# Half of FFN 2's down product from GELU values in two fp32r parts, and new orders of all engines

## The chip, the core and the metric

The kernel runs on one core of a Trainium2 chip. The core's engines are TensorE (PE in the profile; its weight loads are PEld), VectorE (DVE), ScalarE (ACT), GpSimd (POOL) and SyncE (SP), which issues the DMAs. Each engine runs its own instructions in the order in which the program gives them and waits for the others through semaphores. The metric is the device time of one execution in microseconds (us), lower being better.

## The reference, cut to what matters

Four layers, each adding to x (128 sequences, 32 steps, 128 channels). Layer 0, a mixture of experts, comes first; layers 1 to 3 each have a recurrent part over the 32 steps and a feed-forward part (FFN). The change is in FFN 2, and in the order of everything in layers 1 to 3.

```python
x = x + L0_ffn(L0_cond(x))          # experts
x = x + L1_ffn(L1_cond(x))          # LSTM; quantised linear, 3-tap convolution, silu, quantised linear
x = x + L2_ffn(L2_cond(x))          # h = tanh(h @ Wh + x @ Wx + b); the FFN below
x = x + L3_ffn(L3_cond(x))          # gate = sigmoid(h @ Wh.T + z @ Wz.T + b); h = tanh(h * leak + gate * z)

def L2_ffn(x, W1, b1, W2, b2):      # 128 -> 512 -> 128, W1 and W2 ternary (-1, 0, 1)
    h = einsum('bsd,fd->bsf', x, ternary(W1)) + b1
    h = gelu(h, approximate=False)
    return einsum('bsf,df->bsd', h, ternary(W2)) + b2
```

## The kernel before

Everything up to about 318 us of the span is layer 0 with its preparations. The rest, some 235 us, is one fused stage in which the layers 1, 2 and 3 run as a pipeline over the 32 steps t: step t of the LSTM stands beside earlier steps of the later layers. Values are held with channels on the 128 partitions and the 128 sequences along the row.

Steps go in pairs (p, or blocks v of two steps; the last two steps are blocks 15 and 16 of one step each). One loop of the program (`for q in range(FILL, TURNS)`) is called a turn below: two LSTM steps and two steps, or one block, of everything else. What each engine does per turn:

- **TensorE**: `gate_x` and `gate_h` (LSTM gates, lines 1663 and 1673), `turn_h` and `turn_q1` (transposes, 1685 and 1690), `up_tap` (three products per step for the convolution, 1700 and 1701, fp32r), `down1` (bf16, 1709), `turn_y` (1715), `rnn` (layer 2's recurrence, 1722 and 1723), `up2` (FFN 2 up, in two fp32r parts of h2, 1748 and 1749), `down2` (FFN 2 down, 1759, f32), `leaky` (layer 3's recurrence, 1772 and 1773), `mix_products` (1786 and 1787) and `value` (1793).
- **VectorE**: LSTM cell (`gate_products` 1914, `new_cell` 1920, `new_h` 1927), maxima and scales of both quantisations (1933 to 1945, 1980 to 1993), the convolution's three sums per step `conv_next`, `conv_here`, `conv_last` (1951, 1959, 1966), `silu` (1974), the residual sums `new_x2` (1998) and `new_x3` (2003), layer 3's `gated3` (2009) and `leaked3` (2014), and `shift_diff`, `mix`, `gated_value`, `result` (2023 to 2044).
- **ScalarE**: the tanh of every gate and state, both roundings, `scale_y` (1858), `gelu` (1874), `tanh_gate3` (1883) and `tanh_state3` (1888).
- **GpSimd**: `split_h2` alone, once per pair: a cast of h2 to fp32r (2054) and the difference to it (2056).

No scheduler works here. `pe_program`, `act_program` and `dve_program` write the order of each engine out by hand: a prologue, the loop of turns, and an epilogue. An engine that waits at one step holds up all behind it. FFN 2's GELU values lie in one buffer `g2` of 4 x 2 x 128 columns. `down2(v)` writes to bank 3, which `up2` uses too, so `up2(v, 0)` waits for `new_x3(v - 1)` and `gelu(v, ...)` for `down2(v - 1)`. The program has a fixed distance between the LSTM and the later layers: turn q has `gate_h` of steps 2q-3 and 2q-2, `down2(q-7)`, `leaky` of 2q-16 and 2q-15, `mix_products(q-10)` and `value(q-11)`.

## Time and profile before

| | us |
|---|---|
| median of 3 runs | 554.79 (554.44 to 554.80) |
| profiled execution | 554.63 |
| its span (first to last instruction) | 553.3 |
| TensorE busy in the span | 540.1 (98%) |
| VectorE busy | 425.7 (77%) |
| ScalarE busy | 380.6 (69%) |
| GpSimd busy | 197.8 (36%) |

The profiled execution lies 0.16 us under the median. Its span is 1.3 us shorter than its time; this part lies outside the first and last instruction. The TensorE clock was granted in full (1.00 in every stretch shown below). A busy TensorE means that a matmul is in flight; the distance from one matmul's start to the next says what it costs while the engine is saturated. On VectorE and ScalarE, too, the busy times of neighbours overlap by under 0.1 us, so a sum of starts is a little under a sum of busy times.

### The profile page before, as it was taken

Reading aid. Unit: us, or ns where it says so; the run is one execution under the profiler, and the core shown is the slowest. Engines: PE = TensorE matmul, PEld = TensorE weight load, DVE = VectorE, ACT = ScalarE, POOL = GpSimd, SP = SyncE. Lnnn points to the kernel's source line nnn. Section 1 sums busy time; section 2 is a strip of 40 time slices with the busy share of each in tenths; the row PEclk is TensorE's granted clock in tenths of the full one; section 3 lists DMA queues with packets and bytes.
Section 4 is the critical chain, followed back from the end, with each engine's and each line's share of the span. In section 5 each row is a group of like instructions: output and inputs, shape, how many; then the busy total and the mean of one; then the engine's idle time right before and its main releaser. Section 6 shows DMA issues by size and latency. Waiting matters only on the chain.

```text
span 553.3 us, 10078 instructions
## 1 busy us (share of the span) xinstructions
PE 540.1 (98%) x3341; PEld 468.0 (85%) x3341; DVE 425.7 (77%) x1026; ACT 380.6 (69%) x857; POOL 197.8 (36%) x186
## 2 busy tenths in 40 slices
PE   8999999999999999999999989999999999999997
PEld 7877888887887899999999877788989999987785
DVE  4987656567659779676856359998999999999866
ACT  4567767758767664454552246888988888888965
POOL 4688788788788402947100000010000000000100
PEclk9999999999999999999999999999999999999999
DMA  8634306512081302021000000122111111112211
GB/s 285 194 152 159 152 1 230 191 56 97 2 305 43 124 10 82 1 73 62 2 1 1 0 1 2 20 39 21 21 20 20 21 31 30 34 38 47 45 52 39
DMA packets 30227, 37.36 MB, mean 68 GB/s; under 512 B 20096, under 2 KB 23648, under 8 KB 29280
## 3 DMA queue, kind: packets, MB, share of 16 engines
q1 hardware_dynamic: 30176, 36.72, 21.2%
q8 instruction: 28, 0.46, 0.4%
q14 instruction: 23, 0.19, 0.1%
HBM read 30.24 MB, written 2.28 MB: 59 GB/s over the span
## 4 chain that ended last, share of the span: by engine, by line
PE 81%; DVE 12%; ACT 4%; issue 2%; POOL 1%; DVEq 0%; ACTq 0%
PE bank L325 11%; PE bank L1248 10%; PE bank L327 10%; PE bank L326 10%; PE bank L1673 4%; PE bank L1759 4%; PE bank L1663 4%; PE bank L1700 3%; PE bank L1701 3%; PE bank L1316 2%; PE bank L1198 1%; PE bank L1748 1%; PE bank L1786 1%; PE bank L409 1%; PE bank L1772 1%
## 5 line engine op out<-in xcount | busy, mean ns | idle before, releaser
L387 POOL TENSOR_TENSOR hidden_low<-hidden,hidden_high 128x512 fp32r<-128x512 f32 x72 | 94.4, 1318 | 24.6 <-ACT hidden_high L372 22.4
L2054 POOL CAST h_high<-h 128x256 fp32r<-128x256 f32 x15 | 6.4, 426 | 197.6 <-ACT h L1865 191.2
L452 ACT ACTIVATE bank<-bank 128x512 f32<-128x512 f32 x56 | 32.6, 583 | 34.5 <-PE bank L327 34.3
L456 DVE TENSOR_TENSOR hidden<-bank,big 128x512 f32<-128x512 f32 x56 | 38.5, 688 | 15.8 <-ACT bank L452 14.6
L372 ACT CAST hidden_high<-hidden 128x512 fp32r<-128x512 f32 x70 | 43.0, 615 | 3.3 <-DVE hidden L456 1.9
L1700 PE MATMUL bank<-taps_high,q1T 128*128 128x512 f32 x94 | 42.9, 457 | 1.0 <-ACT q1T L1828 0.6
L325 PE MATMUL bank<-xin_high,sw_high 128*128 128x256 f32 x128 | 43.9, 343 | 0.0
L1701 PE MATMUL bank<-taps_low,q1T 128*128 128x512 f32 x94 | 37.1, 395 | 0.0
L1382 DVE COPY yT<-bank 128x256 f32<-128x256 f32 x32 | 13.6, 424 | 30.4 <-PE bank L1248 30.4
L1801 ACT ACTIVATE gates_t<-bank,lstm_b_half 128x128 f32<-128x128 f32 x96 | 28.2, 364 | 12.2 <-PE bank L1673 8.8
L1663 PE MATMUL bank<-x,lstm_wx 128*128 128x128 f32 x256 | 34.4, 277 | 1.7 <-ACT gates_t L1801 0.9
L326 PE MATMUL bank<-xin_low,sw_high 128*128 128x256 f32 x128 | 36.1, 282 | 0.0
L327 PE MATMUL bank<-xin_high,sw_low 128*128 128x256 f32 x128 | 35.9, 280 | 0.0
L1663 PEld LDWEIGHTS bank<-x,lstm_wx 128*128 128x128 f32 x256 | 32.0, 191 | 4.4 <-ACT gates_t L1801 3.3
L1442 ACT ACTIVATE pb<-bank 128x512 f32<-128x512 f32 x32 | 19.5, 608 | 22.7 <-PE bank L327 22.7
L1673 PE MATMUL bank<-hL,lstm_wh 128*128 128x128 f32 x256 | 34.1, 276 | 0.5 <-DVE hL L1927 0.4
L1673 PEld LDWEIGHTS bank<-hL,lstm_wh 128*128 128x128 f32 x256 | 32.3, 192 | 2.4 <-DVE hL L1927 1.4
L998 POOL TENSOR_TENSOR hidden_low<-hidden,hidden_high 128x512 fp32r<-128x512 f32 x24 | 30.8, 1287 | 9.4 <-ACT hidden_high L778 9.0
L1248 PE MATMUL bank<-pb,w 128*128 128x256 f32 x128 | 32.8, 378 | 0.0
L1248 PE MATMUL bank<-th,w 128*128 128x256 f32 x128 | 32.7, 378 | 0.0
L1759 PE MATMUL bank<-g,ffn_w 128*128 128x256 f32 (+1 forms) x136 | 30.7, 368 | 0.0
L1874 ACT ACTIVATE g<-bank,ffn_b 128x256 f32<-128x256 f32 (+1 forms) x68 | 27.6, 467 | 1.0 <-PE bank L1749 0.6
(270 smaller groups left out, 1736.6 us busy)
## 6 DMA issues: line engine op xcount, KB each, us to landing
big<-gates_scratch SPq DMA_DIRECT2D x7, 2048.0 KB, 8.1
w<-in_f_w SPq DMA_DIRECT2D x16, 256.0 KB, 6.2
onehot<-topi_scratch SPq DMA_DIRECT2D x8, 512.0 KB, 4.2
outT<-x SPq DMA_DIRECT2D x15, 128.0 KB, 2.1
xT<-in_xT SPq DMA_DIRECT2D x3, 512.0 KB, 7.4
hidden<-in_ffn_w SPq DMA_DIRECT2D x3, 256.0 KB, 5.2
hidden<-in_conv_w SPq DMA_DIRECT2D x3, 256.0 KB, 4.8
xT<-in_xT SPq DMA_DIRECT2D x2, 256.0 KB, 4.2
```

The costliest lines, as they stand in the source:

```text
L325: pe.matmul(dst, wh[:, cols], vh[:, :], start=start, stop=False)
L326: pe.matmul(dst, wh[:, cols], vl[:, :], start=False, stop=False)
L327: return pe.matmul(dst, wl[:, cols], vh[:, :], start=False, stop=stop)
L372: act.copy(hidden_hl[u % 3][0][:, :], hidden[u % 3][:, :]).then_inc(s_hi, 1)
L387: pool.tensor_tensor(hidden_hl[u % 3][1][:, :], hidden[u % 3][:, :], hidden_hl[u % 3][0][:, :].bitcast(F32), ALU.subtract).then_inc(s_lo, 1)
L456: dve.tensor_tensor(hidden[u % 3][:, :].rearrange("p (i k) -> p i k", k=P), r_bank[j % 2][:, :].rearrange("p (i k) -> p i k", k=P), gate_r ...
L1248: mm = pe.matmul(y_bank[e % 2][:, 0:SLOT_GE], w2[:, e, ht, :], hb[w % 4][:, i * SLOT_GE:(i + 1) * SLOT_GE], start=(ht == 0), stop=(ht == H ...
L1663: mm = pe.matmul(gate_ps(t, q), lstm_wx[:, q * P:(q + 1) * P], x1[:, t, :], start=(0 < t < EARLY or (t > 0 and q == 0)), stop=(t == 0), sk ...
L1673: mm = pe.matmul(gate_ps(t, q), lstm_wh[:, q * P:(q + 1) * P], hL[:, (t - 1) % 2, :], start=(t == 0), stop=(t > 0), skip_group_check=True)
L1700: pe.matmul(dst, q, taps_high[:, 2 - j, :], start=True, stop=False)
L1701: pe.matmul(dst, q, taps_low[:, 2 - j, :], start=False, stop=True).then_inc(c_taps, 1)
L1759: mm = pe.matmul(bank_down(v), ffn2_w2[:, f, :], part(g2[:, f, :, :], v), start=(f == 0), stop=(f == HT - 1))
```

## The change

1. `down2(v)` for blocks 0 to 12 (`SPLIT = 13`): of the four row blocks f of the hidden layer, f = 0 and 1 are multiplied in f32 as before; f = 2 and 3 are multiplied in fp32r twice, once with the rounded GELU values `g2_high` and once with the rest `g2_low`. Blocks 13 to 16 stay in f32.
2. ScalarE makes `g2_high` by one copy of 128x512 per block (`split_g_high`), GpSimd makes `g2_low` by one subtraction of 128x512 (`split_g_low`). The subtraction waits for `g2_high`, for `down2(v - 2)` and for VectorE's `conv_next(2v + 10)`.
3. `g2` becomes a ring of three buffers, so `gelu(v, ...)` waits for `down2(v - 3)` only. `down2(v)` moves from bank 3 to the free half of bank 6, which holds `leaky`'s result: `up2(v, 0)` now waits for `gelu(v - 1, 1)`, not for `new_x3(v - 1)`, and `down2(v)` waits for `new_x3(v - 1)` and for `tanh_gate3` of step 2v - 1.
4. The factor of FFN 1's second weight moves from `m2w` (a VectorE instruction per pair, line 1992, gone) into `new_x2`, which becomes a scalar_tensor_tensor of the same shape.
5. `ffn2_w2` is written as fp32r from a raw copy of its own; f32 products read it through a bitcast.
6. GpSimd no longer splits the one-step pair 15, whose result no product read (`split_h2` for p = 0 to 14).
7. The orders of TensorE, ScalarE and VectorE are written anew. FFN 2's down product and all of layer 3 stand one block later against the LSTM: the loop has `gate_h` of 2q-2 and 2q-1, `down2(q-8)`, `leaky` of 2q-17 and 2q-16, `mix_products(q-11)`, `value(q-11)`.

```diff
@@ up2
                         elif v:
-                            pe.wait_ge(c_x3, v)
+                            pe.wait_ge(c_g2[1], v)
@@ down2
                     pe.wait_ge(c_g2[0], v + 1)
-                    pe.wait_ge(c_g2[1], v + 1)
+                    if v < SPLIT:
+                        pe.wait_ge(c_glow, v + 1)
+                    else:
+                        pe.wait_ge(c_g2[1], v + 1)
+                    if v == 0:
+                        pe.wait_ge(c_to, EARLY)
+                    elif v < PAIRS:
+                        pe.wait_ge(c_x3, v)
+                        pe.wait_ge(c_g3, 2 * v)
                     for f in range(HT):
-                        mm = pe.matmul(bank_down(v), ffn2_w2[:, f, :], part(g2[:, f, :, :], v),
-                                       start=(f == 0), stop=(f == HT - 1))
+                        if v < SPLIT and f >= 2:
+                            pe.matmul(bank_down(v), ffn2_w2[:, f, :], g2_high[:, v % 2, f - 2, :, :], start=False, stop=False)
+                            mm = pe.matmul(bank_down(v), ffn2_w2[:, f, :], g2_low[:, v % 2, f - 2, :, :],
+                                           start=False, stop=(f == HT - 1))
+                        else:
+                            mm = pe.matmul(bank_down(v), ffn2_w2[:, f, :].bitcast(F32), part(g2[:, ring(v), f, :, :], v),
+                                           start=(f == 0), stop=(f == HT - 1))
@@ gelu
-                    if v:
-                        act.wait_ge(c_down, min(v, PAIRS))
+                    if v >= RING:
+                        act.wait_ge(c_down, min(v, PAIRS) - RING + 1)
@@ new steps
+            def split_g_high(v):
+                if 0 <= v < SPLIT:
+                    act.wait_ge(c_g2[1], v + 1)
+                    if v >= 2:
+                        act.wait_ge(c_down, v - 1)
+                    act.copy(g2_high[:, v % 2, :, :, :], g2[:, ring(v), 2:HT, :, :]).then_inc(c_ghigh, 1)
+            def split_g_low(v):
+                if 0 <= v < SPLIT:
+                    pool.wait_ge(c_ghigh, v + 1)
+                    if v >= 2:
+                        pool.wait_ge(c_down, v - 1)
+                    if 2 * v + SPLIT_STEP < T:
+                        pool.wait_ge(c_conv, 3 * (2 * v + SPLIT_STEP))
+                    pool.tensor_tensor(g2_low[:, v % 2, :, :, :], g2[:, ring(v), 2:HT, :, :], g2_high[:, v % 2, :, :, :].bitcast(F32),
+                                       ALU.subtract).then_inc(c_glow, 1)
@@ inverse_hs, new_x2
-                    dve.tensor_scalar(m2w[:, 2 * p:2 * p + 2], m2[:, 2 * p:2 * p + 2], half_ws2[:, 0:1], None, ALU.mult)
-                    dve.tensor_tensor(x1[:, t, :], x1[:, t, :], ps_yT, ALU.add).then_inc(c_x2, 1)
+                    dve.scalar_tensor_tensor(x1[:, t, :], ps_yT, half_ws2[:, 0:1], x1[:, t, :], ALU.mult, ALU.add).then_inc(c_x2, 1)
@@ pe_program, in the loop
-                    down2(q - 7)
+                    down2(q - 8)
@@ pool_program
-                for p in range(PAIRS):
+                for p in range(PAIRS + 1):
                     split_h2(p)
+                    split_g_low(p - 1)
```

TensorE in the middle of a turn, around `down2`, before:

```order
L1663 MATMUL bank0<-x1,lstm_wx 128x128 x4
L1722 MATMUL bank7<-x1,rnn_wx 128x128
L1723 MATMUL bank7<-h2,rnn_wh 128x128
L1759 MATMUL bank3<-g2,ffn2_w2 128x256 x4
L1690 MATMUL bank4<-ident,v1 128x128 x2
L1709 MATMUL bank7<-ffn1_w2,q2T 128x128 x4
```

And the same place of the changed kernel:

```order
L1736 MATMUL bank7<-x1,rnn_wx 128x128
L1737 MATMUL bank7<-h2,rnn_wh 128x128
L1786 MATMUL bank6<-g2,ffn2_w2 128x256 x2
L1782 MATMUL bank6<-g2_high,ffn2_w2 128x256
L1783 MATMUL bank6<-g2_low,ffn2_w2 128x256
L1782 MATMUL bank6<-g2_high,ffn2_w2 128x256
L1783 MATMUL bank6<-g2_low,ffn2_w2 128x256
L1677 MATMUL bank0<-x1,lstm_wx 128x128 x4
L1704 MATMUL bank4<-ident,v1 128x128 x2
L1723 MATMUL bank7<-ffn1_w2,q2T 128x128 x4
```

Two of the four f32 products have become four fp32r ones, `gate_x` (lstm_wx) stands behind `down2` and not ahead of it, and the block that is multiplied here is one earlier.

VectorE in the second half of a turn, around the convolution of an even step, before (`products` and `gates_t` are the LSTM's `gate_products` and `new_cell`, `hL` its `new_h`; `z`, `tap1` and `tap0` are the convolution's sums):

```order
L1951 SCALAR_TENSOR_TENSOR z<-bank1,m1,tap1 128x512
L1914 SCALAR_TENSOR_TENSOR products<-gates_t 128x256
L1998 TENSOR_TENSOR x1<-x1,bank7 128x128
L1920 SCALAR_TENSOR_TENSOR gates_t<-products 128x128
L1959 SCALAR_TENSOR_TENSOR tap1<-bank2,m1,tap0 128x512
L2009 SCALAR_TENSOR_TENSOR p3<-g3,x1 128x128
L1927 SCALAR_TENSOR_TENSOR hL<-gates_t,tc 128x128
```

And in the changed kernel, where GpSimd's new subtraction is let go by the end of the first row:

```order
L1985 SCALAR_TENSOR_TENSOR z<-bank1,m1,tap1 128x512
L1948 SCALAR_TENSOR_TENSOR products<-gates_t 128x256
L1993 SCALAR_TENSOR_TENSOR tap1<-bank2,m1,tap0 128x512
L1954 SCALAR_TENSOR_TENSOR gates_t<-products 128x128
L2000 SCALAR_TENSOR_TENSOR tap0<-bank1,m1,tap_bias 128x512
L2042 SCALAR_TENSOR_TENSOR p3<-g3,x1 128x128
L1961 SCALAR_TENSOR_TENSOR hL<-gates_t,tc 128x128
```

`gates_t` now stands behind a convolution sum, and a second one stands between it and `hL`.

TensorE behind `rnn(31)`, the last step of layer 2's recurrence, before (each pair of `leak_wz` and `leak_wh` is one `leaky`):

```order
L1722 MATMUL bank7<-x1,rnn_wx 128x128
L1723 MATMUL bank7<-h2,rnn_wh 128x128
L1793 MATMUL bank5<-kk,ffn3_wv 128x256
L1772 MATMUL bank6<-x1,leak_wz 128x128
L1773 MATMUL bank6<-h3,leak_wh 128x128
L1751 MATMUL bank3<-h2,ffn2_w1 128x128 x2
L1751 MATMUL bank1<-h2,ffn2_w1 128x128 x2
L1751 MATMUL bank0<-h2,ffn2_w1 128x128 x2
L1786 MATMUL bank5<-xr,ffn3_wr 128x256
L1787 MATMUL bank5<-xk,ffn3_wk 128x256
L1772 MATMUL bank6<-x1,leak_wz 128x128
L1773 MATMUL bank6<-h3,leak_wh 128x128
```

And in the changed kernel:

```order
L1736 MATMUL bank7<-x1,rnn_wx 128x128
L1737 MATMUL bank7<-h2,rnn_wh 128x128
L1799 MATMUL bank6<-x1,leak_wz 128x128
L1800 MATMUL bank6<-h3,leak_wh 128x128
L1765 MATMUL bank0<-h2,ffn2_w1 128x128 x2
L1786 MATMUL bank6<-g2,ffn2_w2 128x256 x4
L1820 MATMUL bank5<-kk,ffn3_wv 128x256
L1799 MATMUL bank6<-x1,leak_wz 128x128
L1800 MATMUL bank6<-h3,leak_wh 128x128
L1813 MATMUL bank5<-xr,ffn3_wr 128x256
L1814 MATMUL bank5<-xk,ffn3_wk 128x256
```

The first `leaky` behind `rnn(31)` was that of step 28 and is that of step 27 now; `down2(14)` has come behind `rnn(31)`.

## Rows read from the trace of the kernel before

**Rows 1.** Windows: busy us and (x instructions) of each engine, clock, DMA.
```profile
core 0: us, PE busy (x) PEld busy (x) DVE busy (x) ACT busy (x) POOL busy (x), PEclk, DMA share, GB/s
317.00:372.20 55.20, 50.92 (x362) 42.95 (x362) 45.88 (x111) 39.78 (x106) 1.33 (x3) 1.00 0.08 15
372.20:492.80 120.60, 120.60 (x871) 108.80 (x870) 112.84 (x287) 106.42 (x287) 12.49 (x20) 1.00 0.15 26
492.80:520.50 27.70, 26.20 (x172) 21.72 (x171) 27.54 (x67) 24.99 (x65) 3.06 (x6) 1.00 0.19 43
520.50:553.40 32.90, 28.29 (x180) 23.68 (x178) 21.11 (x62) 21.57 (x66) 1.58 (x3) 1.00 0.16 45
```
**Rows 2.** Chain that ended last, 384 to 450 us: start, us, what.
```profile
384.65 1.73 PE bank L1759 x8
...
396.72 1.73 PE bank L1759 x8
...
436.38 1.73 PE bank L1759 x8
...
439.07 0.43 PE bank L1793 x2
...
445.16 0.43 PE bank L1786 x2
445.60 0.43 PE bank L1787 x2
...
449.73 1.73 PE bank L1759 x8
```
**Rows 3.** Windows of one early and one full turn; columns as in rows 1.
```profile
384.65:396.72 12.07, 12.07 (x91) 10.98 (x91) 11.47 (x29) 11.00 (x29) 1.12 (x2) 1.00 0.12 24
```
```profile
436.38:449.73 13.35, 13.35 (x97) 12.07 (x97) 12.51 (x33) 11.69 (x33) 1.27 (x2) 1.00 0.18 32
```
**Rows 4.** Timeline of TensorE, 504 us: start, us, instruction (up2's four products).
```profile
504.59 0.28 PE L1748 MATMUL bank<-h_high,ffn_w 128*128 128x256 f32 x1
...
505.06 0.40 PE L1700 MATMUL bank<-taps_high,q1T 128*128 128x512 f32 x1
```
**Rows 5.** Groups by line: out<-in, shapes, xcount, busy us, mean ns.
```profile
L387 POOL TENSOR_TENSOR hidden_low<-hidden,hidden_high 128x512 fp32r<-128x512 f32 x72 | 94.4, 1318 | 24.6 <-ACT hidden_high L372 22.4 <-DVE hidden_high L382 1.1
...
L372 ACT CAST hidden_high<-hidden 128x512 fp32r<-128x512 f32 x70 | 43.0, 615 | 3.3 <-DVE hidden L456 1.9 <-DVE hidden L448 1.0
```
**Rows 6.** Timeline, VectorE and GpSimd, 436 to 438 us.
```profile
436.09 0.22 DVE L1992 TENSOR_SCALAR m2w<-m,half_ws 128x2 f32<-128x2 f32 x1
...
436.22 0.16 DVE L1993 RECIPROCAL sc<-m 128x2 f32<-128x2 f32 x1
...
437.68 0.88 POOL L2056 TENSOR_TENSOR h_low<-h,h_high 128x256 fp32r<-128x256 f32 x1
...
437.88 0.82 DVE L2014 SCALAR_TENSOR_TENSOR pre<-h,leak,p 128x128 f32<-128x128 f32 x1
```
**Rows 7.** Timeline, 502 to 504 us: VectorE beside GpSimd's difference.
```profile
503.06 0.73 POOL L2056 TENSOR_TENSOR h_low<-h,h_high 128x256 fp32r<-128x256 f32 x1
503.30 0.47 DVE L2003 SCALAR_TENSOR_TENSOR x<-bank,ffn_b,x 128x256 f32<-128x256 f32 x1
503.70 0.34 DVE L2014 SCALAR_TENSOR_TENSOR pre<-h,leak,p 128x128 f32<-128x128 f32 x1
```
**Rows 8.** Timeline, 443 to 444 us: `new_h` and the `gate_h` that needs it.
```profile
443.26 0.28 DVE L1927 SCALAR_TENSOR_TENSOR hL<-gates_t,tc 128x128 f32<-128x128 f32 x1
...
444.11 1.06 PE L1673 MATMUL bank<-hL,lstm_wh 128*128 128x128 f32 x8
```
**Rows 9.** Timeline, 480 to 483 us: a `leaky` and its `tanh_gate3`.
```profile
480.77 0.38 PE L1772 MATMUL bank<-x,leak_wz 128*128 128x128 f32 x2
...
480.99 0.39 PE L1773 MATMUL bank<-h,leak_wh 128*128 128x128 f32 x2
...
482.56 0.38 ACT L1883 ACTIVATE g<-bank,leak_b_half 128x128 f32<-128x128 f32 x1
```
**Rows 10.** Timeline of the end: `new_h(31)`, `inverse_hs(15)`, `rnn(31)`, `leaky` 28 and 31, last sum.
```profile
496.69 0.28 DVE L1927 SCALAR_TENSOR_TENSOR hL<-gates_t,tc 128x128 f32<-128x128 f32 x1
...
519.02 0.16 DVE L1993 RECIPROCAL sc<-m 128x2 f32<-128x2 f32 x1
...
537.48 0.39 PE L1723 MATMUL bank<-h,rnn_wh 128*128 128x128 f32 x2
538.14 0.38 PE L1772 MATMUL bank<-x,leak_wz 128*128 128x128 f32 x2
...
545.57 0.46 PE L1772 MATMUL bank<-x,leak_wz 128*128 128x128 f32 x2
...
551.38 0.29 DVE L2044 TENSOR_TENSOR x<-x,o 128x128 f32<-128x128 f32 x1
```

More of the change, by code:

```diff
@@ L2605, in dve_program @@
+                inverse_hs(4)
+                conv_here(11)
+                conv_last(11)
+                gated3(0)
+                new_x2(6)
+                conv_next(12)
+                leaked3(0)
+                gate_products(15)
+                conv_here(12)
+                new_cell(15)
+                conv_last(12)
+                new_h(15)
+                silu(5)
                 for q in range(FILL, TURNS):
-                    mix(q - 10, xr, mu_r, c_xr)
-                    gate_products(2 * (q - 2))
```

697 lines of the change are left out of this document (396 added, 301 removed).

## The prediction

> **What bounds the kernel now.** I read three views in this order. First the windows of the fused stage [rows 1]: between 372.2 and 492.8 us TensorE is busy 120.60 us of 120.60, VectorE 112.84, ScalarE 106.42, at a clock of 1.00 throughout. In the filling stage before it, TensorE is idle 55.20 - 50.92 = 4.3 us; from 492.8 to 520.5 us VectorE is the full one (27.54 of 27.70) and TensorE idles 1.5 us; in the last 32.9 us nobody is full (28.29, 21.11, 21.57). Second, the chain that ended last [rows 2]: in the middle it lies on TensorE alone, and `down2` comes back every 13.35 us (436.38 to 449.73), its first products lasting 1.73 us. A turn is what TensorE's own instructions add up to. That is shown by the early turns: without `mix_products` (0.43 + 0.43) and `value` (0.43) the turn is 12.07 us (384.65 to 396.72), and 12.07 + 1.29 = 13.36. So the middle is a sum of matmuls, and whatever leaves TensorE there leaves the time, until another engine is full. Third, the full turn's window [rows 3]: VectorE 12.51 and ScalarE 11.69 us of 13.35. These are the two that can become full.
>
> **The fp32r half of `down2`.** Eight f32 passes take 1.73 us [rows 2], so half of them takes 0.865. Four fp32r products of 128x256, `up2`'s, take 505.06 - 504.59 = 0.47 us [rows 4], with the same weights-to-columns shape as the new ones. A block saves 0.865 - 0.47 = 0.395 us, 13 blocks save **5.1 us**. All 13 lie before `rnn(31)` on TensorE, where it is full or nearly so; 9 of them stand in the loop of turns. A full turn becomes 13.35 - 0.40 = 12.95 us. Ends: were all fp32r products that follow f32 ones to cost 0.1 more, 3.8 us; nothing makes them cheaper.
>
> **The split's copies.** ScalarE gets 13 casts of 128x512 at 0.615 us [rows 5], 8.0 us in all; in a full turn 11.69 + 0.62 = 12.3 of 12.95. Nothing on the path, while the order fits; what is late if it doesn't is the tanh behind it. GpSimd gets 13 differences of 128x512 at 1.32 us [rows 5], 17 us on an engine that works 1.27 us of a full turn [rows 3]. `down2(v)` needs it, but by the orders about 9 us of TensorE's work lie between the `up_tap` that feeds the releasing `conv_next` and `down2(v)`; 0.75 of convolution and 1.32 of difference fit in easily. Price 0.
>
> **What the difference does to VectorE.** GpSimd's difference ran from 437.68 to 438.56, and `leaked3`, a VectorE instruction that reads two SBUF tiles, took 0.82 us from 437.88, ending just behind it; beside no difference it takes 0.34 [rows 6, 7]. `new_x3`, which reads one operand from PSUM, ran beside another difference in its usual 0.47 [rows 7]. So the first kind stands still until GpSimd is done, the second does not. The new difference starts when `conv_next` ends, and `gate_products`, two convolution sums and `new_cell` come next. The sums read PSUM. `new_cell` reads SBUF alone and comes some 0.66 us behind `gate_products`; the difference, 1.32 us long, can hold it up by 0 to 0.65 us. On the other side the old hold-up of 0.48 (0.82 - 0.34) at `leaked3` should go: `mix` and the scales that now follow `new_h` fit before the cast and difference of h2. With `m2w` gone (0.22) VectorE's turn is 12.51 - 0.48 - 0.22 = 11.8, plus at most 0.65: 12.5 of 12.95. Price 0 in the middle. For the LSTM the reserve is thin: today `hL` is ready at 443.54 and `gate_h` starts at 444.11, 0.57 us later [rows 8]. I take 0, with 0 to 0.1 per turn inside my range.
>
> The Trainium skill (SBUF — State Buffer, "Who interferes with whom") calls this pair of ports an exclusive lock: a VectorE instruction with two SBUF inputs and a GpSimd instruction that reads SBUF block each other for the whole instruction, whichever begins second. The trace agrees (0.82 against 0.34). It speaks against the change where the difference is longer than the convolution sum beside it; by that rule alone `new_cell` waits out the full 0.65.
>
> **`m2w`.** It costs 436.22 - 436.09 = 0.13 us from start to start, 16 times [rows 6]. It counts only where VectorE is full: some four pairs while filling and two at 492.8 to 520.5. **-0.5 us** (0 to -1). `new_x2` keeps shape and PSUM operand: 0.
>
> **One block later.** `down2`, two `leaky`, `mix_products` and `value` of one block leave the part up to the last LSTM step and come behind it: 1.33 + 0.88 + 0.87 + 0.43 = 3.5 us of TensorE, taken off here and added there (a `leaky` is two pairs of passes of 480.99 - 480.77 = 0.22 us, so 0.44 [rows 9]). While TensorE is full this is neutral. It is not neutral at two places. First, the three or four early turns: TensorE's work there falls to 12.07 - 0.40 - 0.44 = 11.2 us, while ScalarE's 11.00 [rows 3] becomes 11.0 + 0.62 - 0.38 = 11.2 (a `tanh_gate3` less) and VectorE's is 11.47 - 0.7 - 0.34 (a `leaked3` less) + 0.65 = 11.1. They are level, and an in-order engine without reserve waits: 0.3 us a turn, **+1.0 us** (0 to +2). Second, the end. From the second half of `rnn(31)` (537.48) to the end of the last sum (551.67) are 14.2 us; the four `leaky` from 28 to 31 come 2.5 us apart (538.14 to 545.57) [rows 10]. In the new order `leaky(27)` is the first behind `rnn(31)`: five in a row, so this piece becomes 14.2 + 2.5 = 16.7. The 3.5 us less before it pay that. VectorE's chain from `new_h(31)` to `inverse_hs(15)` is 22.4 us of full work now [rows 10]; the new order has 21.5 in the same piece by the same durations. I take for the end together **-0.5 us** (-2.5 to +2).
>
> **The filling** stage is bound by the LSTM's latency and then by VectorE; the first twelve steps keep their distances, and only a few `up_tap` change places. 0 (-0.5 to +0.5). The preparation on GpSimd has the same number of instructions; 0.
>
> **The new waits.** `down2(v)` waits for `tanh_gate3(2v-1)`. Behind it queue `gate_x` and the whole of TensorE. Today `tanh_gate3` ends up to 2.2 us after its `leaky` starts (480.77 to 482.94 [rows 9]); the new order has `leaky` 0.44, `up_tap` 0.47, `up2` 0.47 and `rnn` 0.44 ahead of `down2`: 1.8 us. By the old lag `down2` would wait 0.3 us a turn. In ScalarE's new order `tanh_gate3` stands right behind `tanh_gates`, which are done before `leaky` starts, not behind `quantise_hs` (1.16 us) as at 482. I take 0; the upper end is 9 x 0.3 = +2.7. The relaxed waits of `up2` and `gelu` take nothing off, since TensorE has no idle time there.
>
> **Sum.** 554.63 - 5.1 - 0.5 + 1.0 - 0.5 = 549.5 us for the profiled execution, 549.7 by the median, which is 0.16 higher.
>
> **Rivals.**
> - *Another engine fills up* (0.20): ScalarE or VectorE, with 0.65 and 0.45 us of reserve, or the wait for `tanh_gate3`, sets the turn at about 13.15 and not 12.95. For: reserves under 5% in in-order queues. Against: VectorE sits idle 0.84 us and ScalarE 1.66 us of today's turn (13.35 less 12.51 and 11.69 [rows 3]) and TensorE never waits for either. Nine turns give 1.8 back, the end 1 more: 551 to 553.3.
> - *The end gains more* (0.12): TensorE idles some 6 us between 492.8 and 553.4 today (1.5 + 4.6); if the shorter VectorE chain lets the conv end sooner and part of that closes, 2 to 3 us more: 546.8 to 548.2.
> - *The change does nothing* (0.07): the turn stays at 13.35 because the LSTM's loop, through the held-up `new_cell`, is its new bound. Savings outside the turns offset the dearer early ones: about 554.5.
> - *Slower* (0.08): the difference starts ahead of `gate_products`, so that this waits 1.32 us and `new_cell` behind it too. `hL` then comes 1.3 us late; with the reserve of 0.57 [rows 8] `gate_h` starts 0.75 us late in each turn. From 0.40 us per turn on this eats the saving; at 0.75 it costs 9 x 0.35 = 3 us more than it saves: about 557.
>
> **How the numbers follow.** The forecast itself (0.53) covers 548.2 to 551. Forecast, first and second rival hold 0.85 and reach from 546.8 to 553.3, which is my range. A measurement of this kernel tells about 0.2% (1.1 us) from no change. Faster: 0.53 + 0.20 + 0.12 = 0.85; the same 0.07; slower 0.08.
>
> **What would show it.** In the changed kernel's profile: `down2` with 0.86 us for its f32 half and 0.47 for the four fp32r products, and coming back every 12.95 us in the chain of waits, which stays on TensorE; at 13.2 or more the first rival is right, and the idle time ahead of `gate_h`, `down2` or `mix_products` names the engine. `new_cell` at up to 0.9 us in place of 0.28 where the difference runs; `gate_products` at 1.3 would be the slower case. `leaked3` back at 0.34. The piece from `rnn(31)` to the last sum at 16.7 us. The forecast is wrong if TensorE has idle time in the middle, or if the fp32r products are over 0.12 us apart.

## The result, and the profile after

The changed kernel takes **557.94 us** (median of 5, 556.74 to 558.67) against 554.79 (median of 5), a ratio of 1.0059 with a 95% interval of 1.0043 to 1.0074. It is 3.1 us slower; the prediction was 549.7 us. The profiled execution took 557.99 us, its span is 556.6.

Windows of the changed kernel, cut at the places that answer to [rows 1] (filling, full turns up to `gate_h(31)`, two pieces behind it); columns as there:

```profile
core 0: us, PE busy (x) PEld busy (x) DVE busy (x) ACT busy (x) POOL busy (x), PEclk, DMA share, GB/s
317.00:371.00 54.00, 50.34 (x347) 41.66 (x348) 44.91 (x103) 38.02 (x102) 1.13 (x2) 1.00 0.05 12
371.00:486.60 115.60, 115.08 (x859) 104.58 (x858) 112.58 (x271) 107.44 (x294) 23.69 (x29) 1.00 0.15 28
486.60:519.00 32.40, 28.32 (x174) 23.42 (x173) 29.98 (x65) 27.74 (x68) 6.80 (x8) 0.95 0.15 37
519.00:556.60 37.60, 32.13 (x204) 26.97 (x202) 24.24 (x72) 23.61 (x74) 3.59 (x5) 1.00 0.15 40
```

The middle is as foretold: the LSTM's last step starts at 486.8, 6.0 us earlier than the 492.8 of before, with TensorE busy 115.08 of 115.60 us. The loss comes out behind it. Before, 60.5 us followed that step; now 69.8 us do. By the order some 3.9 of the 9.3 us are work of the later layers that now stands behind the step (`down2` 1.33, two `leaky` 0.88, `mix_products` 0.87 and two `value` 0.86 us), less 1.2 us that the split takes off blocks 10 to 12 there; the other 6.6 us are waiting and a slower clock. TensorE sits idle 4.1 + 5.5 = 9.6 us of these (before 1.5 + 4.6 [rows 1]), and its clock is 0.95 in the first piece.

One full turn, the answer to the second of [rows 3]:

```profile
442.10:455.05 12.95, 12.95 (x98) 11.83 (x97) 12.73 (x32) 11.99 (x34) 2.49 (x3) 1.00 0.21 32
```

The chain of waits inside it: `down2`'s f32 half, its four fp32r products, and `gate_x` (start, us, what):

```profile
445.39 0.86 PE bank L1786 x4
446.26 0.12 PE bank L1782
446.38 0.12 PE bank L1783
446.49 0.12 PE bank L1782
446.61 0.12 PE bank L1783
446.73 0.89 PE bank L1677 x8
```

0.86 and 0.47 us, in place of the 1.73 of [rows 2]. The new difference on GpSimd (L2098) and the VectorE instructions beside it in a full turn, from the timeline:

```profile
438.15 1.31 POOL L2098 TENSOR_TENSOR g_low<-g,g_high 128x512 fp32r<-128x512 f32 x1 [2.90 <-DVE z L1985]
...
438.23 0.74 DVE L1993 SCALAR_TENSOR_TENSOR tap<-bank,m,tap 128x512 f32<-128x512 f32 x1
...
438.89 0.71 DVE L1954 SCALAR_TENSOR_TENSOR gates_t<-products 128x128 f32<-128x128 f32 x1
439.52 0.74 DVE L2000 SCALAR_TENSOR_TENSOR tap<-bank,m,tap_bias 128x512 f32<-128x512 f32 x1
```

`new_cell` (gates_t) takes 0.71 us and ends soon after the difference; usual is 0.28. The turn has room for that. In the early turns it is held longer, 1.26 us at block 0's difference (from 377.02) and 0.97 at block 3's (from 412.87); e8 below shows what that costs. Blocks 11 and 12 are another case, and I had not looked at them: the wait for `conv_next(2v + 10)` is written only where such a step exists, 2v + 10 < 32, so their differences start as soon as ScalarE's copy is there. Block 11's, with what stands around it on four engines:

```profile
507.74 0.73 POOL L2089 TENSOR_TENSOR h_low<-h,h_high 128x256 fp32r<-128x256 f32 x1
507.80 0.95 DVE L2063 SCALAR_TENSOR_TENSOR xr<-diff,mu_r,h 128x256 f32<-128x256 f32 x1
...
508.43 1.45 POOL L2098 TENSOR_TENSOR g_low<-g,g_high 128x512 fp32r<-128x512 f32 x1
...
508.67 1.48 DVE L2063 SCALAR_TENSOR_TENSOR xk<-diff,mu_k,h 128x256 f32<-128x256 f32 x1
...
510.15 0.46 DVE L2036 SCALAR_TENSOR_TENSOR x<-bank,ffn_b,x 128x256 f32<-128x256 f32 x1
...
510.67 0.49 PE L1799 MATMUL bank<-x,leak_wz 128*128 128x128 f32 x2 [1.25 <-DVE x L2036]
...
512.24 0.45 PE L1736 MATMUL bank<-x,rnn_wx 128*128 128x128 f32 x1 [0.86 <-DVE x L2031]
```

Two mixes take 0.95 and 1.48 us (0.47 when free). The first stands beside `h_low`, the second beside the new difference. `new_x3` behind them comes late, and TensorE waits 1.25 us for it and 0.86 us for the next `new_x2`. Only the second mix and the 1.25 us belong to block 11's difference: e3 below, where that difference is held back, has the first mix at 0.95 and the wait of 0.86 all the same. What follows on TensorE, as windows:

```profile
500.00:512.80 12.80, 10.23 (x65) 8.50 (x65) 12.50 (x26) 10.56 (x24) 3.83 (x4) 0.98 0.12 31
512.80:516.20 3.40, 3.40 (x17) 2.86 (x17) 1.55 (x5) 2.19 (x5) 0.00 (x0) 0.56 0.07 17
516.20:530.00 13.80, 12.76 (x90) 11.05 (x88) 9.74 (x27) 12.10 (x34) 3.59 (x5) 1.00 0.30 64
```

For some 3.4 us the granted clock is near half, the lower of the two levels (1.2 GHz); TensorE is busy all that time and gets little done. The trace of before has the full clock from `gate_h(0)` to its last matmul. Of the five executions of the changed kernel the one at a mean clock of 1.000 took 556.74 us, the others (0.992 to 0.997) 557.7 to 558.7, so the fall goes with 1 to 2 us here.

The end, the answer to [rows 10]: `rnn(31)` (L1737), `leaky` 27 right behind it, `leaky` 31, last sum:

```profile
536.23 0.39 PE L1737 MATMUL bank<-h,rnn_wh 128*128 128x128 f32 x2
536.47 0.46 PE L1799 MATMUL bank<-x,leak_wz 128*128 128x128 f32 x2
...
547.62 0.43 PE L1799 MATMUL bank<-x,leak_wz 128*128 128x128 f32 x2
...
554.65 0.29 DVE L2077 TENSOR_TENSOR x<-x,o 128x128 f32<-128x128 f32 x1
```

`rnn(31)` is only 1.25 us ahead of before, and from there to the end of the last sum are 18.7 us (before 14.2). From `leaky` 27 to 31 are 11.15 us, 2.8 per step (before 7.43 us for three, 2.5 each [rows 10]), and from `leaky(31)` to the end 7.3 us (before 6.1).

A correction to the list of parts ahead of the prediction: its item 6 is wrong. The kernel before made 15 splits of h2 as well (its `h_high` has 15 instances in the trace), so that item changes nothing.

### The profile page after: what moved, and what is told of

Read it like the earlier page. It is cut to its first block, busy times and chain, and to the rows that moved or that the text cites. A ratio compares the mean times of both kernels' runs of the same rounds, so it can differ in the third digit from the quotient of the medians.

```text
span 556.6 us, 10122 instructions
## 1 busy us (share of the span) xinstructions
PE 539.9 (97%) x3341; PEld 467.3 (84%) x3341; DVE 430.1 (77%) x1010; ACT 384.9 (69%) x870; POOL 215.1 (39%) x199
## 4 chain that ended last, share of the span: by engine, by line
PE 78%; DVE 12%; ACT 4%; issue 3%; POOL 1%; DVEq 0%; ACTq 0%
PE bank L327 11%; PE bank L1250 10%; PE bank L329 10%; PE bank L328 10%; PE bank L1687 4%; PE bank L1677 3%; PE bank L1714 3%; PE bank L1715 3%; PE bank L1786 2%; PE bank L1318 2%; PE bank L1200 1%; PE bank L1813 1%; PE bank L627 1%; DVE hs L2008 1%; PE bank L1820 1%
## 5 line engine op out<-in xcount | busy, mean ns | idle before, releaser
L389 POOL TENSOR_TENSOR hidden_low<-hidden,hidden_high 128x512 fp32r<-128x512 f32 x72 | 94.5, 1320 | 24.6 <-ACT hidden_high L374 22.4
L1714 PE MATMUL bank<-taps_high,q1T 128*128 128x512 f32 x94 | 44.4, 472 | 0.7 <-DVE z L1985 0.5
L2098 POOL TENSOR_TENSOR g_low<-g,g_high 128x512 fp32r<-128x512 f32 x13 | 17.4, 1340 | 30.9 <-DVE z L1985 30.9
```

The source lines that it names most:

```text
L389: pool.tensor_tensor(hidden_hl[u % 3][1][:, :], hidden[u % 3][:, :], hidden_hl[u % 3][0][:, :].bitcast(F32), ALU.subtract).then_inc(s_lo, 1)
L1714: pe.matmul(dst, q, taps_high[:, 2 - j, :], start=True, stop=False)
```

## The experiments

All kernels of a group ran on one chip beside runs of the kernel before: e1 to e4; e5 to e8; e9 to e12; e13 to e16. Across groups the ratios are to be compared, with their 95% intervals, and not the times. A trace is one execution, and its time can lie up to 1.2 us from its kernel's median (e1 below). The start of the fused stage differs by up to 1 us between traces, so the traces are compared from the start of `gate_h(0)` on. These are start times read from the traces, us after `gate_h(0)`, the last column the end of the last sum:

```
kernel                 gate_h(31)  rnn(31)  leaky(31)  last sum   against before
before                   172.7      217.2     225.5     231.6
after                    166.6      215.8     227.4     234.7        +3.1
e1_order_only            168.9      216.3     227.9     235.3        +3.7
e2_split11               166.4      214.3     225.9     233.2        +1.6
e3_guard11               166.4      213.9     225.5     232.8        +1.2
e4_first_half            172.5      218.0     226.3     232.5        +0.9
e5_m2w_back              168.5      217.3     228.9     236.2        +4.6
e6_middle_only           170.0      214.4     222.7     228.8        -2.8
e7_after_middle_only     166.5      214.4     226.0     233.3        +1.7
e8_no_guard              165.5      212.9     224.5     232.9        +1.3
e9_blocks_1_to_10        170.1      215.0     223.3     229.4        -2.2
e10_part4_alone          172.5      217.2     225.6     231.7        +0.1
e11_with_part4           169.8      215.0     223.3     229.4        -2.2
e12_h_low_free           170.7      215.6     223.9     230.0        -1.6
e13_vector_tail          172.7      219.2     227.5     233.6        +2.0
e14_vector_middle        172.7      217.2     225.5     232.2        +0.6
e15_tensor_tail          172.7      218.8     227.1     233.2        +1.6
e16_less_vector_tail     169.0      215.0     226.6     234.0        +2.4
```

### e1_order_only: the new orders without the split

The kernel after with `SPLIT` at 0: no two-part products, copies or differences.

```diff
-            SPLIT, SPLIT_STEP = 13, 10
+            SPLIT, SPLIT_STEP = 0, 10
```

> The changed kernel with SPLIT = 0: all of down2 in f32 as before, no copy on ScalarE and no difference of GELU values on GpSimd; the ring of three buffers, bank 6, the new x2 sum and the new orders stay. Theory A (the GELU differences of blocks 11 and 12, which wait for no convolution, hold up VectorE in the end; TensorE idles behind it and its clock falls to half for 3.4 us): the fp32r gain of 13 x 0.395 = 5.1 us is lost, some 3.5 us of lock and clock come back: 559.5 us. Theory B (the new order costs the time by itself, in the end above all): nothing comes back, 562 to 563 us. In both the turn is 13.35 us again.

558.62 us (median of 4, 557.46 to 560.04), ratio 1.0077 (1.0051 to 1.0104), less than either theory expected. The new order by itself costs 3.7 us by the trace, which is that of the fastest of the four, and 4.3 by the ratio. It does so behind `gate_h(31)`, which comes 3.8 us earlier than before. The split, taken away, is worth no more than 0.5 us in the changed kernel (0.7 by the medians).

### e2_split11 and e3_guard11: the differences of blocks 11 and 12

e2 leaves their split out, e3 keeps it and lets block 11's difference wait for the last `conv_next`:

```diff
@@ e2_split11
-            SPLIT, SPLIT_STEP = 13, 10
+            SPLIT, SPLIT_STEP = 11, 10
@@ e3_guard11, in split_g_low
                     if 2 * v + SPLIT_STEP < T:
                         pool.wait_ge(c_conv, 3 * (2 * v + SPLIT_STEP))
+                    elif v == 11:
+                        pool.wait_ge(c_conv, 3 * T - 3)
```

> The changed kernel with SPLIT = 11: blocks 11 and 12 go back to f32, so that no difference runs on GpSimd after the last guarded one. TensorE gets 2 x 0.395 = 0.8 us more. Theory A (the two unguarded differences start the loss in the end): the sums xr and xk at 508 us take 0.48 us each again (now 0.95 and 1.48), TensorE's clock stays full: 557.9 - 1.6 - 1.7 + 0.8 = 555.4 us. Theory B (the order): 558 to 558.7 us.

> The changed kernel with one wait more: the difference of block 11 waits for conv_next(31), so that it runs beside conv_here(31). Theory A: as with blocks 11 and 12 in f32 but without TensorE's 0.8 us: 554.6 us, clock full. Theory B: 557.9 us as without it.

556.06 us (1.0025, 1.0014 to 1.0037) and 556.01 us (1.0026, 1.0014 to 1.0037), both 1.9 us less than the changed kernel, and the clock is 1.000 in both traces. The same place in e3:

```profile
507.37 0.95 DVE L2063 SCALAR_TENSOR_TENSOR xr<-diff,mu_r,h 128x256 f32<-128x256 f32 x1
...
508.24 0.47 DVE L2063 SCALAR_TENSOR_TENSOR xk<-diff,mu_k,h 128x256 f32<-128x256 f32 x1
...
509.23 0.49 PE L1799 MATMUL bank<-x,leak_wz 128*128 128x128 f32 x2 [0.24 <-DVE x L2036]
...
510.81 0.49 PE L1736 MATMUL bank<-x,rnn_wx 128*128 128x128 f32 x2 [0.86 <-DVE x L2031]
```

The second mix is back at 0.47 us and TensorE's wait for `new_x3` at 0.24: 1.0 us of the 1.9 is that hold, the other 0.9 comes behind it, where the clock no longer falls. The first mix, beside `h_low`, is held in e2 and e3 too, against what e2's expectation took. Block 12's difference has no such wait in e3 either, so the loss is block 11's. It is not the whole loss, and e3 with two blocks more in two parts (0.79 us less TensorE work) is no faster than e2 by the medians and 0.4 us by the traces: the split earns little or nothing there. Against e1, the same order without it, the 13 blocks of e3 are worth 2.4 us by the traces.

### e4_first_half: the split in the order before

The order, banks and buffers of the kernel before; the products f = 0 and 1 of blocks 0 to 10 in two parts, the copy behind `gelu(v, 0)`, the difference behind `split_h2`, with no wait beside VectorE's work.

```diff
-                        mm = pe.matmul(bank_down(v), ffn2_w2[:, f, :], part(g2[:, f, :, :], v),
+                        if v < SPLIT and f < 2:
+                            pe.matmul(bank_down(v), ffn2_w2[:, f, :], g2_high[:, v % 2, f, :, :], start=(f == 0), stop=False)
+                            pe.matmul(bank_down(v), ffn2_w2[:, f, :], g2_low[:, v % 2, f, :, :], start=False, stop=False)
@@ act_program, in the loop
                     tanh_gates(2 * q)
+                    split_g_high(q - 6)
@@ pool_program
                     split_h2(p)
+                    split_g_low(p)
```

> The kernel before, its orders kept, with the fp32r split alone: the first half (f = 0 and 1) of blocks 0 to 10, since its GELU values are ready some 4.8 us ahead of down2; the copy stands behind tanh_gates on ScalarE, the difference behind split_h2 on GpSimd. TensorE saves 11 x 0.395 = 4.3 us. If the loss is in the new order or in the end (theories A and B alike): 550.5 us, turn 12.95 us. If the split's copy and lock are what costs (a third theory, C): 553 us or more, with TensorE waiting in the turns.

555.11 us, ratio 1.0008 (0.9997 to 1.002): no gain, as the third theory had it. Its timeline (of an execution 0.8 us above the median) shows why. A scale of 128x2 at block 0's difference:

```profile
371.22 1.27 POOL L2085 TENSOR_TENSOR g_low<-g,g_high 128x512 fp32r<-128x512 f32 x1 [8.18 <-ACT g_high L1898]
...
371.65 0.87 DVE L1959 TENSOR_SCALAR m<-mx 128x2 f32<-128x2 f32 x1
```

and `leaked3(18)` at block 10's:

```profile
498.73 1.28 POOL L2085 TENSOR_TENSOR g_low<-g,g_high 128x512 fp32r<-128x512 f32 x1 [6.78 <-ACT g_high L1898]
...
498.99 1.18 DVE L2034 SCALAR_TENSOR_TENSOR pre<-h,leak,p 128x128 f32<-128x128 f32 x1
500.09 1.21 DVE L2000 TENSOR_REDUCE mx<-hs 128x2 f32<-128x1024 f32 x1
```

0.87 us for an instruction of 0.16, 1.18 for one of 0.34. Against before, steps fall back by 1.2 us around the first place and by 1.1 us around the second, and by 0.5 us in between, where the same scale is held for 0.93 and 0.94 us at the differences of blocks 1 and 2. From there to the second place each turn gains 0.25 us and not 0.39.

### e6, e12 and e9: the split in the order before, with its differences placed

e6 splits only blocks 3 to 9 and makes `h_low` wait for `new_x3` of the block before, so that it stands beside a convolution sum and not beside `leaked3`. e12 is e6 without that wait. e9 is e6 with blocks 1 to 10.

```diff
@@ e6_middle_only, against e4_first_half
-            SPLIT = 11
+            SPLIT_FROM, SPLIT = 3, 10
@@ split_h2, ahead of h2_low
+                    if SPLIT_FROM <= p <= SPLIT:
+                        pool.wait_ge(c_x3, p)
@@ e9_blocks_1_to_10, against e6
-            SPLIT_FROM, SPLIT = 3, 10
+            SPLIT_FROM, SPLIT = 1, 11
@@ split_g_low, ahead of g2_low
+                    if v == SPLIT - 1:
+                        pool.wait_ge(c_pre3, 2 * v - 1)
```

> The order of the kernel before, with the two-part product only for blocks 3 to 9, those whose turns have TensorE busy without a gap, and with GpSimd's h_low difference held until new_x3 of the block before has been written, so that it stands beside a convolution instead of beside leaked3. Everything is computed. Theory A (what the split earns is 0.25 to 0.395 us for each block in the full turns and nothing elsewhere; what e4_first_half lost, 1.2 us around 372 and 1.1 us around 499, were holds of VectorE by the GELU differences of blocks 0 and 10 beside step_h and leaked3): turns of 12.95 to 13.1 us, gate_h(31) 1.8 to 2.8 us ahead of before, 552.0 to 553.2 us, faster than both kernels. Rival (the tail gives back whatever comes early, and the split earns nothing at the end of the program): gate_h(31) ahead by as much, the last sum not, 554.3 to 555.2 us.

> e6_middle_only without its wait of h_low for new_x3: GpSimd's h_low difference stands beside leaked3 again, as in the kernel before, and only the GELU differences are new. Everything is computed. e4_first_half gave back 0.14 of each 0.39 us in the full turns. If that is leaked3 held by h_low (theory A), the turn is 13.1 us and the time 1.0 us more than e6's, 553.7. If the wait for new_x3 does nothing, 552.7.

> e6_middle_only with the two-part product for blocks 1 to 10 instead of 3 to 9, h_low held to new_x3 in all of them, and the difference of block 10 held until leaked3(18) has been written. Everything is computed. Theory A (a block's split is worth its 0.39 us wherever TensorE is the engine waited for and no VectorE instruction with both operands in SBUF is held): TensorE is busy without a gap from 372 us of the span on, so blocks 1, 2 and 10 bring up to 3 x 0.39 = 1.2 us more, 551.5 us, counted from e6's 552.7. Rival (the turns of 12.1 us around blocks 1 and 2 have no room for the copy and the difference): 552.7 to 553.7 us, no better than e6.

e6: **552.66 us, ratio 0.9961 (0.9939 to 0.9984), faster than both kernels.** Its executions took 551.7 to 554.0 us, but for one of 1079.3, and the trace is of one with 551.8. By that trace the end is 2.8 us earlier, and 7 blocks x 0.395 is 2.8: the whole saving arrives there; by the ratio it is 2.2 us (0.9 to 3.4). A turn of e6, then of e12:

```profile
442.01:454.99 12.98, 12.98 (x99) 11.80 (x97) 12.07 (x34) 12.10 (x34) 2.47 (x3) 1.00 0.17 32
```

```profile
443.36:456.48 13.12, 13.12 (x99) 11.88 (x98) 12.53 (x33) 12.23 (x34) 2.61 (x3) 1.00 0.19 31
```

In e6 `leaked3` is free and `h_low` stands beside a convolution sum that it does not disturb; the GELU difference stands beside `max_hs`, a reduction:

```profile
449.15 0.34 DVE L2034 SCALAR_TENSOR_TENSOR pre<-h,leak,p 128x128 f32<-128x128 f32 x1
...
449.81 0.74 DVE L1979 SCALAR_TENSOR_TENSOR tap<-bank,m,tap 128x512 f32<-128x512 f32 x1
...
450.03 0.73 POOL L2078 TENSOR_TENSOR h_low<-h,h_high 128x256 fp32r<-128x256 f32 x1 [1.16 <-DVE x L2023]
...
457.55 1.35 POOL L2087 TENSOR_TENSOR g_low<-g,g_high 128x512 fp32r<-128x512 f32 x1 [6.79 <-ACT g_high L1898]
...
457.66 1.21 DVE L2000 TENSOR_REDUCE mx<-hs 128x2 f32<-128x1024 f32 x1
```

e12: 553.5 us (0.9978, 0.9968 to 0.9987), turn 13.12. The one held `leaked3` (0.82 us, as in [rows 6]) costs 0.14 us a turn and by the traces 1.2 us in all (0.9 by the ratios, whose intervals overlap).

e9: 552.37 us (0.9963, 0.9952 to 0.9974), by the trace 0.6 us behind e6. Blocks 1, 2 and 10, with the waits that came with them, bring nothing, where 1.2 us was expected: the rival's number was right. Its turn from `down2(1)` to `down2(2)`:

```profile
384.12:396.14 12.02, 12.02 (x93) 10.67 (x92) 11.68 (x27) 10.97 (x30) 2.40 (x3) 1.00 0.12 24
```

It is 12.02 us long, against 12.07 in [rows 3], though 0.39 us of matmul time is gone, and TensorE still shows as busy for all of it: some matmuls now start 0.3 us after the one ahead that followed it by 0.1 before (`leaky` behind `turn_y`: 394.07 and 394.36). So a full TensorE in this view does not prove that TensorE sets the turn. VectorE is busy 11.68 us of it, which leaves 0.34; in e6's full turn it is 12.07 of 12.98.

The Trainium skill (SBUF — State Buffer, "Who interferes with whom") sorts VectorE's instructions in the same way: two SBUF inputs are blocked beside a GpSimd instruction that reads SBUF, and so is a tensor_scalar in a 2-port mode beside GpSimd; one SBUF input outside these modes is not, and on trn2 a tensor_reduce never is. The traces agree: 1.18 and 0.87 us against 0.34 and 0.16 for the first two, 0.74 and 1.21 us unchanged for the last two. Which mode the scaling ran in, no trace shows.

### e7_after_middle_only: which blocks earn in the order after

```diff
@@ against e3_guard11
-            SPLIT, SPLIT_STEP = 13, 10
+            SPLIT_FROM, SPLIT, SPLIT_STEP = 3, 10, 10
```

> The order after, with the differences of the late blocks held to a convolution as in e3_guard11, and with the two-part product only for blocks 3 to 9 instead of 0 to 12. Everything is computed. If only blocks of the full turns earn anything (theory A), this is as fast as with all 13 blocks, 555.5 to 556.4 us (556.0 there). If each of the 13 earns its 0.395 us (the prediction's count), six fewer cost 2.4 us: 558.4 us.

556.22 us, ratio 1.0025 (1.0005 to 1.0045); e3, with 13 blocks, had 1.0026. Seven blocks earn what thirteen do (by the traces 1.9 us against e1 where thirteen earn 2.4; the prediction's count puts 2.4 us between the two kernels).

### e8_no_guard: the wait that sets the difference beside the convolution

```diff
@@ against e2_split11, in split_g_low
-                    if 2 * v + SPLIT_STEP < T:
-                        pool.wait_ge(c_conv, 3 * (2 * v + SPLIT_STEP))
```

> The kernel after with the split only for blocks 0 to 10 (556.06 us in e2_split11) and without the wait that sets GpSimd's difference beside VectorE's convolution: it starts as soon as the copy is made and the h_low difference is done. Everything is computed. If the wait is what keeps VectorE out of TensorE's way in the full turns (rival), the difference meets the mix, leaked3 or new_x2 there, the turn is longer than 12.95 us, up to 13.35, and the time 556.5 to 558.6. If VectorE has room for one hold per turn (theory A, for the middle), the turn stays 12.95 and the time 555.6 to 556.5; a loss can then only come from a block outside the full turns.

555.13 us, ratio 1.0003 (0.9984 to 1.0022), 0.9 us less than e2 (whose interval overlaps), better than both theories. The difference now starts by itself where nothing is held, and `new_cell` is back at 0.28:

```profile
433.72 1.28 POOL L2096 TENSOR_TENSOR g_low<-g,g_high 128x512 fp32r<-128x512 f32 x1
...
434.21 0.74 DVE L2000 SCALAR_TENSOR_TENSOR tap<-bank,m,tap_bias 128x512 f32<-128x512 f32 x1
...
437.40 0.28 DVE L1954 SCALAR_TENSOR_TENSOR gates_t<-products 128x128 f32<-128x128 f32 x1
```

The turn is 12.96 us either way. By the traces the gain lies in the early turns, where `new_cell` is no longer held (0.9 us by `gate_h(31)`, and all of it is there by `gate_h(20)`), and 0.5 us more come by `rnn(31)`; the end gives 1.1 back under a fallen clock. The wait that the change added costs about 0.9 us and protects nothing that a run shows.

### e5_m2w_back and e10_part4_alone: part 4

```diff
@@ e5_m2w_back, against e3_guard11
+                    dve.tensor_scalar(m2w[:, 2 * p:2 * p + 2], m2[:, 2 * p:2 * p + 2], half_ws2[:, 0:1], None, ALU.mult)
-                    dve.scalar_tensor_tensor(x1[:, t, :], ps_yT, half_ws2[:, 0:1], x1[:, t, :], ALU.mult, ALU.add).then_inc(c_x2, 1)
+                    dve.tensor_tensor(x1[:, t, :], x1[:, t, :], ps_yT, ALU.add).then_inc(c_x2, 1)
```

e10 is the kernel before with the same lines the other way round.

> e3_guard11 (556.0 us) with part 4 of the change undone: m2w and its multiplication are back, 16 times 0.13 us on VectorE, and new_x2 is again a tensor_tensor, 32 times 0.07 us less. Everything is computed. By these two sums VectorE has the same to do (2.1 against 2.2 us): 555.7 to 556.4 us. The prediction's figure for part 4, a gain of 0.5 us from taking m2w away at the same new_x2, would make it 556.5.

> The kernel before with part 4 of the change alone: m2w gone, new_x2 multiplies by the constant half_ws2. Everything is computed. On e3_guard11 the same part was worth 3.0 us, because m2w stood beside h_low there and took 0.69 us. In the order before it stands free (0.22 us): theory A expects 554.3 to 555.2 us, no difference. If the part is worth something by itself (the rival, and the prediction's 0.5 us): 552 to 554.3.

e5: 558.99 us, ratio 1.0073 (1.0052 to 1.0095), 3.0 us more than e3 (2.6 by the ratios), where no difference was expected. e10: 554.16 us, ratio 0.9998 (0.9989 to 1.0006), nothing. In the new order `m2w`, a 128x2 scaling, stands beside `h_low`:

```profile
435.32 0.78 POOL L2090 TENSOR_TENSOR h_low<-h,h_high 128x256 fp32r<-128x256 f32 x1
...
435.44 0.69 DVE L2026 TENSOR_SCALAR m2w<-m,half_ws 128x2 f32<-128x2 f32 x1
```

and e5's turn is 13.10 us with VectorE busy for all of it:

```profile
441.94:455.04 13.10, 13.10 (x100) 11.84 (x97) 13.10 (x33) 12.00 (x34) 2.49 (x3) 1.00 0.14 32
```

The expectation counted 0.13 us per instruction from the order before; held, it is 0.6. Part of the 3.0 us is once more a fallen clock behind the LSTM (0.70 at 512 to 516 us of e5's span).

### e11_with_part4

e9 with part 4 of the change, the lines as under e10.

> e9_blocks_1_to_10 with part 4 of the change too. Everything is computed. The same as e9_blocks_1_to_10 within 0.5 us by theory A, 0.5 to 3 us faster by the rival that m2w is held there too.

552.15 us, ratio 0.9963 (0.995 to 0.9977), the same as e9. In the order before `m2w` is held nowhere in the full turns.

### e13, e14, e15 and e16: whose work is paid behind the LSTM

[rows 1] has VectorE busy 27.54 of 27.70 us behind `gate_h(31)`. e13 and e14 add the same four VectorE instructions, there and in four full turns. e15 adds four f32 matmuls there. e16 is e1 with VectorE work left out there: nine operations touch one column of 128 only, so its output is not the reference's.

```diff
@@ e13, e14: the spare instruction, k = 0 to 3
+                    dve.scalar_tensor_tensor(spare_out[:, k, :], spare_in[:, :], 1.0, spare_in[:, :], ALU.mult, ALU.add)
@@ e15, down2
+                    if v in (10, 11):
+                        for _ in range(2):
+                            pe.matmul(bank_down(v), ffn2_w2[:, 0, :], part(g2[:, 0, :, :], v), start=True, stop=True)
@@ e16, against e1: mix and result touch n columns
+                    n = 1 if v in (7, 8, 9) else N
+                    n = 1 if v in (5, 6, 7) else N
```

> The kernel before with four spare VectorE instructions (128x512, about 0.66 us from start to start) in the stretch behind gate_h(31), 505 to 518 us of the span. All of the reference is computed, and 2.6 us of VectorE work besides. Theory D (behind gate_h(31) VectorE is the engine waited for, 27.54 of 27.70 us busy, so that what an order puts there or holds there is paid in full): 556.8 to 557.6 us, 2 to 2.8 more than before. Rival (the wait there is for TensorE or for chains between the engines): under 1 us more, 554.8 to 555.8.

> The kernel before with the same four spare VectorE instructions, one in each of the turns q = 12 to 15, where TensorE is busy without a gap. All of the reference is computed, and 2.6 us of VectorE work besides. Theory D: VectorE has 0.6 us to spare in such a turn, so 554.8 to 555.2 us. Rival (VectorE's work costs the same wherever it stands): 557.4.

> The kernel before with two spare fp32 matmuls of 256 columns (0.43 us each) ahead of down2(10) and of down2(11), in the same stretch, 1.7 us of TensorE work in all, overwritten by the product proper. All of the reference is computed. Theory D (TensorE is not the engine waited for there, and what a split saves of it there is not paid out): under 0.9 us more, 554.8 to 555.7. Rival (TensorE's work is paid in full there too, as the prediction's 13 times 0.395 us took it): 556.5.

> e1_order_only (the order after without the split, 558.6 us) with VectorE work left out behind gate_h(31): the mixes of blocks 7 to 9 and the additions of result of blocks 5 to 7 touch one column of 128 only, about 2.7 us less. Left out are the other columns of these nine operations. Theory D (the new order costs what it does because it leaves about one more block of FFN 3 on VectorE behind gate_h(31)): 2 to 3 us less, 555.6 to 556.6. Rival (the new order's price is TensorE's own: latencies between its pieces, blocks that come late in a chain): under 1 us less, 557.6 or more.

- e13: 556.45 us, ratio 1.0038 (1.0024 to 1.0051), +2.1 us for 2.6 us of VectorE work.
- e14: 554.63 us, ratio 1.0001 (0.999 to 1.0012), nothing for the same work in the full turns. Its trace runs with that of before up to the last `mix_products`; the 0.6 us in the table come behind it, from 549 us on, where its clock is 0.52.
- e15: 556.88 us, ratio 1.004 (1.0024 to 1.0056), +2.2 us for 1.7 us of TensorE work (by the trace +1.6).
- e16: 557.33 us, ratio 1.0052 (1.0038 to 1.0065), 1.3 us less than e1 by the traces for about 2.7 us of VectorE work, between its theory and its rival; the ratios' intervals overlap.

The same stretch of e13 and of e15 in windows:

```profile
492.80:520.50 27.70, 24.57 (x158) 20.04 (x156) 27.66 (x64) 23.67 (x60) 3.03 (x4) 1.00 0.19 42
```

```profile
492.50:520.20 27.70, 26.59 (x169) 22.25 (x168) 26.17 (x61) 24.14 (x60) 2.30 (x4) 1.00 0.19 44
```

The theory that VectorE alone is waited for there is half right. Its work is paid there at 0.8 of its length and in the full turns at nothing. TensorE's is paid too, nearly in full. Both have little idle time there (TensorE 1.5 us of 27.70, VectorE 0.2 [rows 1]), and a microsecond more on either one comes out at the end.

## Why the prediction was wrong

Three runs take the 3.2 us of the traces apart. The new order without the split costs 3.7 us (e1), the split's 13 blocks give 2.4 back once block 11's difference is out of the way (e3 against e1), and that difference costs 1.9 (the changed kernel against e3). The prediction had 0 (-0.5 + 1.0 - 0.5), 5.1 and 0 for the three, which makes its miss of 8.2 us.

By the traces the ledger can also be written in TensorE's terms, as an estimate. Work is the sum of its steps at their usual lengths (`gate_h` 0.89, `up_tap` 0.465, `down2` 1.73 or 1.335 and so on); waiting is the time from `gate_h(0)` to the last `mix_products` less that work:

```
kernel             work   waiting to gate_h(31)   waiting behind it
before            210.9         10.6                    8.4
after             205.8         12.3                   15.0
e1_order_only     210.9         11.1                   11.6
e3_guard11        205.8         12.2                   13.2
e6_middle_only    208.1         10.6                    8.4
```

The work column has the saving of 5.1 us in it by the measured lengths of `down2`. Against it, 1.7 us of waiting came before `gate_h(31)`, 6.6 us behind it: -5.1 + 1.7 + 6.6 = +3.2 us.

- **Durations and the full turn: right.** 0.395 us per block, turn 12.95 us, `new_cell` held 0.71 us, `leaked3` back at 0.34, clock full in the middle, no wait at `down2` for `tanh_gate3`. Both copies were free in the middle.
- **"All 13 lie before `rnn(31)` on TensorE, where it is full or nearly so": the step that made the saving too large.** Hardly more than blocks 3 to 9 earn (e7, e9). In the new order they bring 1.9 us and all 13 together 2.4, not 5.1; in the old order they bring 2.8. Around block 0 to 2 and behind `gate_h(31)` a saved matmul goes into waiting. e15 shows that adding TensorE work there is paid; so the likely reason is that the split's own copy and difference, and the hand-over to `down2`, take back what its matmuls save. That was not tested by itself.
- **"I take for the end together -0.5 us": the largest miss.** e1 shows +3.2 us of waiting behind `gate_h(31)` from the order alone. I had compared one VectorE chain by its length (21.5 against 22.4 us) and priced a fifth `leaky` at 2.5 us. The chain from `rnn(31)` to the end is 18.7 us, not 16.7: the `leaky` come 2.8 us apart and not 2.5, and behind `leaky(31)` stand 7.3 us and not 6.1, with `mix_products(14)` now behind it and not ahead of it. And the work taken off in front (3.5 us by my count; it is 0.4 more, since `value` moved by two blocks) did not move `rnn(31)` by 3.5 but by 0.9 in e1. e13 and e15 tell why such work is not neutral: in this stretch both engines' time is paid, so a block that is pushed into it costs time there. e16 wins 1.3 us of e1's 3.7 back by leaving VectorE work out. Which hand-overs hold the other 2.4 us stays open.
- **"Price 0" for the hold-ups: right in the middle, wrong for block 11 and in the early turns.** Block 11's is 1.9 us with the fallen clock (e3). The condition 2v + 10 < 32 stood in the diff. In the early turns `new_cell` is held by up to 0.98 us (1.26 less 0.28), not by at most 0.65; letting the difference go by itself wins about 0.9 us there (e8).
- **One block later, early turns: +1.0 was expected.** Up to `gate_h(31)` e1 has 0.5 us more waiting than before and the changed kernel 1.7. So the order cost half of the estimate, and the split cost 1.2 there; 0.9 of it is the added wait beside the convolution (e8).
- **`m2w` -0.5: nothing by itself** (e10). I overlooked that `new_x2` is dearer as a scalar_tensor_tensor reading PSUM, 0.34 us against 0.27, 32 times. Together with the new order it is worth about 3 us (e5), because it takes away an instruction that GpSimd would hold.
- **The rivals.** None names what happened. The slower one put the loss into the full turns, where there was none, so that its 557 lies near the measured time is chance; "another engine fills up" was right that reserves are thin, in the wrong stage.

In the order before, e6 bears out the prediction's mechanism for the full turns: seven blocks, 2.8 us by the trace, 552.66 us.

## What to carry to other kernels

A saving on an engine is paid out in full only in the stages where that engine is busy without a gap and the next engine has more room than the saving (in e9's early turn VectorE had 0.34 us for a saving of 0.39, which makes it the likely limit there); count the instances per stage, not over the whole loop. Where two engines are both nearly full, as behind the last step of the first layer here, work moved in is paid whichever of them has it, so leave the order of such a stretch alone or measure it by itself with one spare instruction. Before a difference is put on GpSimd, list which VectorE instruction runs beside each instance, those of the epilogue too: here sums that read PSUM and reductions were good neighbours (0.74 and 1.21 us, unchanged), sums of two SBUF operands and even tiny scalings were not (1.18 for 0.34, 0.87 for 0.16).
